# Mixing products of 33 rows and the decay's second product in pairs of row halves, two banks at a time

## The reference, cut to what matters

```
xa = ln(x);  sx = shift(xa) - xa
t  = tanh((xa + sx * maa_x) @ maa_w1).reshape(B, L, 5, 32)
mw, mk, mv, mr, mg = einsum('blfd,fdc->blfc', t, maa_w2)     # five products over only 32 rows
xw = xa + sx * (maa_w + mw)   ... the same for k, v, r, g
w  = exp(-exp(time_decay + tanh(xw @ decay_w1) @ decay_w2))  # the last product is over 64 rows
r, k, v = xr @ Wr.T, xk @ Wk.T, xv @ Wv.T;  g = silu(xg @ Wg.T)
for each token:  a = k v^T;  out = r (faaaa a + s);  s = a + w s
y = groupnorm(out);  x = x + (y * g) @ Wo.T
xc = ln(x);  x = x + sigmoid(xr2 @ fWr.T) * (relu(xk2 @ fWk.T)^2 @ fWv.T)
```

## Time and profile before

| | |
|---|---|
| median of 3 runs | 4260.67 us (4258.37 to 4265.11) |
| the profiled execution | 4252.74 us, its span 4250.9 us |
| busy over the span: TensorE, VectorE | 3730.4 us (88%), 2998.0 us (71%) |
| busy: ScalarE, GpSimd | 2057.8 us (48%), 1742.2 us (41%) |
| mean granted clock of TensorE | 0.954 of 2.4 GHz |

### The profile page before, as it was taken

One profiled execution on the slowest core, in us unless ns is written; L12 is line 12 of the kernel. 1 busy time (PEld: TensorE's weight loads), 2 busy tenths in 40 slices (PEclk: granted clock), 3 DMA queues, 4 the chain that ended last, 5 costly groups with the idle time before them and its releaser, 6 DMA issues. The chain is left out here.

```text
span 4250.9 us, 71399 instructions
## 1 busy us (share of the span) xinstructions
PE 3730.4 (88%) x21636; PEld 2882.3 (68%) x21636; DVE 2998.0 (71%) x6732; ACT 2057.8 (48%) x5384; POOL 1742.2 (41%) x1210
## 2 busy tenths in 40 slices
PE   5998998588888886999999778999999999999976
PEld 4777777477777774899999655666666666666643
DVE  5777777477777775556556338888888878888872
ACT  4777777367777675545545322333333333333322
POOL 2444444144444441000000135666666666666652
PEclk9999999799999997999999889999999999999988
DMA  3434434344444443010010210000000000000000
GB/s 110 104 99 109 104 99 104 96 116 118 104 114 110 122 104 116 30 44 30 30 41 33 73 50 18 24 24 23 24 23 24 23 24 23 24 23 23 23 18 15
DMA packets 146611, 256.58 MB, mean 60 GB/s; under 512 B 27184, under 2 KB 32048, under 8 KB 145424
## 3 DMA queue, kind: packets, MB, share of 16 engines
q1 hardware_dynamic: 146448, 254.49, 22.0%
HBM read 107.62 MB, written 33.55 MB: 33 GB/s over the span
## 5 line engine op out<-in xcount | busy, mean ns | idle before, releaser
L1201 POOL TENSOR_TENSOR c_S<-c_S,c_rT 128x1024 f32<-128x1024 f32 x256 | 558.1, 2180 | 458.4 <-DVE c_S L1479 417.6
L1479 DVE TENSOR_TENSOR_SCAN c_S<-c_wT,c_s,c_vb 128x256 f32<-128x256 f32 x1024 | 709.0, 734 | 45.0 <-issue 2.7
L1474 DVE TENSOR_TENSOR c_vb<-c_kT,c_vb 128x512 f32<-128x512 f32 x512 | 352.4, 688 | 286.4 <-PE c_vb L1645 255.6
L348 POOL TENSOR_TENSOR x_prob<-x_prob,x_rsums 128x512 f32<-128x512 f32 x256 | 275.2, 1075 | 477.7 <-DVE x_rsums L510 477.7
L348 POOL TENSOR_TENSOR s_prob<-s_prob,s_rsums 128x512 f32<-128x512 f32 x256 | 275.2, 1075 | 431.0 <-DVE s_rsums L510 431.0
L1645 PE MATMUL c_vb<-c_vhl,c_spread 128*128 128x512 f32 x512 | 300.4, 597 | 73.6 <-DVE c_S L1479 60.6
L404 ACT ACTIVATE x_prob<-x_t,x_tmin 128x256 f32<-128x256 f32 x512 | 256.4, 502 | 218.3 <-DVE x_tmin L503 218.0
L404 ACT ACTIVATE s_prob<-s_t,s_tmin 128x256 f32<-128x256 f32 x512 | 256.5, 502 | 193.9 <-DVE s_tmin L503 193.6
L862 PE MATMUL b_ps<-b_ln_high,b_w_high 128*128 128x256 f32 x1024 | 290.9, 284 | 14.8 <-DVE b_ln_low L804 14.8
L863 PE MATMUL b_ps<-b_ln_low,b_w_high 128*128 128x256 f32 x1024 | 290.8, 284 | 0.0
L864 PE MATMUL b_ps<-b_ln_high,b_w_low 128*128 128x256 f32 x1024 | 290.8, 284 | 0.0
(11 more groups left out here) (266 smaller groups left out, 10572.4 us busy)
## 6 DMA issues: line engine op xcount, KB each, us to landing
s_stack<-s_parts_qk SPq DMA_DIRECT2D x384, 128.0 KB, 2.4
x_stack<-x_parts_qk SPq DMA_DIRECT2D x384, 128.0 KB, 2.4
s_x_in<-in_x SPq DMA_DIRECT2D x16, 512.0 KB, 3.6
s_xb<-in_x SPq DMA_DIRECT2D x16, 512.0 KB, 4.1
x<-s_x_out SPq DMA_DIRECT2D x16, 512.0 KB, 4.8
x_enc<-in_ctx SPq DMA_DIRECT2D x16, 512.0 KB, 4.4
x_x_in<-x SPq DMA_DIRECT2D x16, 512.0 KB, 3.7
x_xb<-x SPq DMA_DIRECT2D x16, 512.0 KB, 4.1
```

Source lines behind the costliest of these rows:

```text
L348: nc.gpsimd.tensor_tensor(prob[:, h % 4, :, :], prob[:, h % 4, :, :], rsums[:, h, :].unsqueeze(2).to_broadcast([P, TC, T]), ALU.mult).then ...
L1201: nc.gpsimd.tensor_tensor(S[:, n % 4, :, 0:T], S[:, n % 4, :, 0:T], rT[:, par, :, :], ALU.mult).then_inc(z_ready, 1)
L1474: nc.vector.tensor_tensor(pair(vb, i), pair(kT[:, par, :, :], i), pair(vb, i), ALU.mult)
L1479: op = nc.vector.tensor_tensor_scan(S[:, n % 4, c, 1:T + 1], wT[:, par, c, :], vb[:, c, :], s0[:, par, c, n:n + 1], ALU.mult, ALU.add)
```

## The change

It does four things. (1) The pieces of `tT` and `mix2` move: each mixing matrix has 33 rows, and starts at row 0 (w, r, g) or row 64 (k, v); `dec1` writes its result to rows 64 to 127 and `dec2` runs there. (2) Two units, one of each row half (mw with mk, mr with mv, mg with dec2), are issued together by `fill_together`, alternating between two banks. (3) `FILLS` is reordered, so that such units are neighbours: mk joins mw in step 0, k0 and k1 move to the end of step 2 and the start of step 3, mr and mv stand in step 4, mg and dec2 in step 8, xcT and v0 in step 9, g0 in step 11; GpSimd's `sxc` moves from step 8 to 9 and its addition for g from step 7 to 8. (4) `t` is split into 128 and 32 columns, and its tanh is taken in five pieces of 32 rows.

```diff
-    FILLS = {0: (["g1"], ["mw0", "mw1"]), 1: (["mk0", "mk1"], ["y0", "y1"]), 2: (["dec1"], ["mr0", "mr1"]),
-             3: (["k0"], ["dec20", "dec21"]), 4: (["zT0", "zT1"], ["k1"]), 5: (["o0"], ["mv0", "mv1"]),
-             6: (["r0"], ["o1"]), 7: (["r1"], ["mg0", "mg1"]), 8: (["bonus0", "bonus1"], ["xcT0", "xcT1"]),
-             9: (["v0"], []), 10: (["v1"], ["g0"]), 11: (["kk0"], []), 12: (["kk1"], []),
-             13: (["xaT0", "xaT1"], ["rr0"]), 14: (["rr1"], ["kv0"]), 15: (["kv1"], ["t"])}
+    FILLS = {0: (["g1"], ["mw0", "mk0", "mw1", "mk1"]), 1: ([], ["y0", "y1"]), 2: (["dec1"], ["k0"]), 3: (["k1"], []),
+             4: (["zT0", "zT1"], ["mr0", "mv0", "mr1", "mv1"]), 5: (["o0"], []), 6: (["o1"], ["r0"]), 7: (["r1"], []),
+             8: (["bonus0", "bonus1"], ["mg0", "dec20", "mg1", "dec21"]), 9: (["xcT0", "xcT1"], ["v0"]), 10: (["v1"], []),
+             11: (["kk0"], ["g0"]), 12: (["kk1"], []), 13: (["xaT0", "xaT1"], ["rr0"]), 14: (["rr1"], ["kv0"]),
+             15: (["kv1"], ["t"])}
+    TOGETHER = {"mk0": "mw0", "mk1": "mw1", "mv0": "mr0", "mv1": "mr1", "dec20": "mg0", "dec21": "mg1"}
+    MIX_AT = {"w": (0, 0), "k": (2 * DM, 0), "v": (2 * DM, 1), "r": (0, 2), "g": (0, 1)}
...
-                    if n == 8:
+                    if n == 9:
                         pool.wait_ge(emptied["act"], units.emptied(k + 2, "xcT1"))
                         nc.gpsimd.tensor_tensor(sxc[:, :, :], xcT[:, :, 0:T], xcT[:, :, 1:T + 1],
...
-                        if "front" in parts and n in (0, 1, 4, 5, 7):
-                            add_xa(k, MIX[(0, 1, 4, 5, 7).index(n)])
+                        if "front" in parts and n in (0, 1, 4, 5, 8):
+                            add_xa(k, MIX[(0, 1, 4, 5, 8).index(n)])
...
-                        nc.scalar.activation(tT[0:3 * DM, 0, :], unit(name)[0:3 * DM, 0:T], ACT.Tanh)
-                        nc.scalar.activation(tT[0:2 * DM, 1, :], unit(name)[0:2 * DM, T:2 * T], ACT.Tanh).then_inc(done, 1)
+                        for j, n in enumerate("wkvrg"):
+                            row, place = MIX_AT[n]
+                            op = nc.scalar.activation(tT[row:row + DM, place, :], channels(name)[DM * j % P:DM * j % P + DM, DM * j // P, :],
+                                                      ACT.Tanh)
+                        op.then_inc(done, 1)
...
+                def few_rows(name, a):
+                    c = 2 * int(name[-1]) + a
+                    row, place = (DD, 2) if name[:-1] == "dec2" else MIX_AT[name[1]]
+                    if name[:-1] == "dec2":
+                        rows, moving = DD, decT[:, :]
+                    else:
+                        rows, moving = DM + 1, tT[:, place, :]
+                    return nc.tensor.matmul(channels(name)[:, a, :], mix2[row:row + rows, place, c * P:(c + 1) * P],
+                                            moving[row:row + rows, :], start=True, stop=True)
+
+                def fill_together(k, name, second):
+                    if name == "mw0":
+                        pe.wait_ge(emptied["act"], units.emptied(k + 1, "t"))
+                        pe.wait_ge(mix2_loaded, 16 * NMIX * (KC + 1))
+                    if second == "dec20":
+                        pe.wait_ge(emptied["act"], units.emptied(k + 2, "dec1"))
+                        weights("decay_w2")
+                    few_rows(name, 0)
+                    few_rows(second, 0)
+                    few_rows(name, 1).then_inc(filled, 1)
+                    few_rows(second, 1).then_inc(filled, 1)
+
                 def take(k, names, parts, par):
                     for name in names:
                         reader, value = units.before(k + 2, name)
                         pe.wait_ge(emptied[reader], value)
-                        if part_of(name) in parts:
+                        if name in TOGETHER.values() and part_of(name) in parts:
+                            continue
+                        if name in TOGETHER and part_of(name) in parts:
+                            fill_together(k, TOGETHER[name], name)
+                        elif part_of(name) in parts:
                             fill(k, name, 1 - par)
```

More of the change, by code:

```diff
@@ L990, in phase_c @@
         centred = sb("centred", P, 2, P)
-        mix2 = sb("mix2", P, NMIX, C)
-        w = {**w, **{n: sb(n, P, *shape) for n, shape in WEIGHTS_C.items()}}
+        mix2 = sb("mix2", P, 3, C)
+        w = {**w, **{n: sb(n, P, *shape) for n, shape in WEIGHTS_C.items() if n != "decay_w2"}}
         acc = ctx.enter_context(nc.psum_tensor("c_acc", [P, KC, T], F32))
@@ L1085, in load_weight @@
                 def load_weight(n):
-                    rows = d[n].shape[0]
-                    dst = g2T[:, :, :, :].rearrange("p a (c b) n -> p (a c) (b n)", b=2) if n == "Wv" else w[n][0:rows]
+                    dst = mix2[DD:2 * DD, 2, :] if n == "decay_w2" else w[n][0:P]
+                    if n == "Wv":
+                        dst = g2T[:, :, :, :].rearrange("p a (c b) n -> p (a c) (b n)", b=2)
                     sp.dma_start(dst, d[n]).then_inc(weights_loaded[n], 16)
@@ L1092, in _ @@
                 for j in range(NMIX):
-                    place = DM * j if j < 3 else DM * (j - 3)
-                    sp.dma_start(mix2[place:place + DM, j, :],
+                    row, place = MIX_AT["wkvrg"[j]]
+                    sp.dma_start(mix2[row:row + DM, place, :],
                                  d["maa_w2"][DM * j % P:DM * j % P + DM, DM * j // P, :]).then_inc(mix2_loaded, 16)
                     at = COL_AT["maa_" + "wkvrg"[j]]
-                    ones = 3 * DM if j < 3 else 2 * DM
                     for c in range(KC):
-                        sp.dma_start(mix2[ones:ones + 1, j, c * P:(c + 1) * P],
+                        sp.dma_start(mix2[row + DM:row + DM + 1, place, c * P:(c + 1) * P],
                                      d["cols"][:, at + c:at + c + 1].rearrange("p o -> o p"),
@@ L1525, in weights @@
                         pe.wait_ge(weights_loaded[name], 16)
-                    return w[name]
+                    return w.get(name)
                 def transposed(out, src, c):
@@ L1569, in fill @@
                         pe.wait_ge(xxx_ready, k + 3)
-                        for to, n0, n in ((0, 0, 3 * DM), (1, 3 * DM, 2 * DM)):
+                        for to, n0, n in ((0, 0, P), (1, P, NMIX * DM - P)):
                             for c in range(KC):
@@ L1573, in fill @@
                                                       xmix[:, 0, c, :], start=(c == 0), stop=(c == KC - 1))
-                    elif what in ("mw", "mk", "mr", "mv", "mg"):
-                        if name == "mw0":
-                            pe.wait_ge(emptied["act"], units.emptied(k + 1, "t"))
-                            pe.wait_ge(mix2_loaded, 16 * NMIX * (KC + 1))
-                        j = "wkvrg".index(what[1])
-                        rows = 3 * DM + 1 if j < 3 else 2 * DM + 1
-                        for a in range(2):
-                            c = 2 * i + a
-                            op = nc.tensor.matmul(u[:, a, :], mix2[0:rows, j, c * P:(c + 1) * P], tT[0:rows, j // 3, :],
-                                                  start=True, stop=True)
                     elif name == "dec1":
@@ L1586, in fill @@
                         for c in range(KC):
-                            op = nc.tensor.matmul(u[0:DD, 0, :], weights("decay_w1")[:, c, :], xmix[:, 1, c, :],
+                            op = nc.tensor.matmul(u[DD:2 * DD, 0, :], weights("decay_w1")[:, c, :], xmix[:, 1, c, :],
                                                   start=(c == 0), stop=(c == KC - 1))
-                    elif what == "dec2":
-                        pe.wait_ge(emptied["act"], units.emptied(k + 2, "dec1"))
-                        for a in range(2):
-                            c = 2 * i + a
-                            op = nc.tensor.matmul(u[:, a, :], weights("decay_w2")[0:DD, c * P:(c + 1) * P], decT[:, :],
-                                                  start=True, stop=True)
                     elif what == "bonus":
```

6 lines of the change are left out of this document (3 added, 3 removed).

## The result

The changed kernel takes 4428.14 us (median of 4 runs, 4411.97 to 4429.77), the kernel before 4259.76 beside it: ratio 1.0384, 95% interval 1.0358 to 1.0410. The direction was as forecast, the size was not: +168 us where +65 was said, and 50 us above the range.

The account below looks back on a forecast made before the run. No engine bounds it throughout: TensorE's queue is late in about half the steps, VectorE busy through the others. 4.2 us lost plus 0.1 for the clock, over 15 passes, gave +65 and 4325 us; range 4272 to 4378.

Parts of the forecast that it names:

- Overlap of pairs: Mixing products and dec2 in separate row halves run together on TensorE, saving 5.1 us a pass (bounds 0 and 5.1).
- rival "no overlap": Pairs in row halves don't run together; +35 us on the forecast, 4360 us; chance 0.13.
- g1's bank: Step 0: pair 2 and broadcast 1.0 wait for VectorE's read of g1; half 1.0 at +8.2 instead of +6.5.
- k moved ahead: Steps 2 to 5: k0 waits for GpSimd's sum, and k0, k1 hold broadcasts 3.0, 3.1; half 3.1 5.8 us late.
- o0 set by GpSimd's gating: Around half 5.0: o0 waits for GpSimd's gating, late by k's chain, and starts at +35.9.
- Steps 5 to 9 win back 3.1: Products of mv and mg gone from steps 5 to 7, VectorE sets the pace; half 9.0 only 1.4 us late.
- the walk: Step-by-step timing of one pass from g1's first product; loss 4.2 us a pass, perhaps 2.5 too long.
- second chain: Steps 9 to 13: xcT0 waits for mg0's bank, GpSimd's difference moves later; kk0 at +74.1 instead of +70.6.
- Clock, +0.1 us a pass: Idle stretches of TensorE move more than they multiply, so granted clock costs +0.1 us a pass; bounds -0.9 and +1.7.
- rival "clock": Clock falls at k0 and a second place in each pass, 1.7 us each; +51 us, 4376 us; chance 0.12.
- the two terms that could lengthen the time: Upper bounds over 15 passes: no overlap on pair 2 and the mg/dec2 group, +35 us; the clock, +24 us.

Follow-up runs that it names:

- c_order_only: Kernel before with the changed kernel's order of fills and GpSimd's two steps that go with it, each unit as before, no pairs: 4419.09 us, 1.0378.
- i_same_rows: Changed kernel with both partners of each pair in the same row half, so that nothing runs side by side: 4515.07 us, 1.0617.
- p_own_waits: i_same_rows with partners taken apart, each unit waiting for its own bank alone and filled at once: 4502.13 us, 1.0590.
- o_all_rows: i_same_rows with mixing products over 128 rows, 64 for r, zero coefficients in the rows added: 4505.77 us, 1.0586.
- m_pairs_64: Changed kernel with mixing products over 64 rows instead of 33, zero coefficients in the rows added: 4413.59 us, 1.0362.
- b_pair_late: Changed kernel with the second pair of step 0 (mw1, mk1) moved behind broadcast 1.0, to step 1: 4422.69 us, 1.0396.
- e_k_apart: Changed kernel with k0 and k1 each one list later, behind broadcasts 3.0 and 3.1: 4367.70 us, 1.0248.
- a_read_first: Changed kernel with VectorE reading mr and mv ahead of half 5.0 instead of behind it: 4360.96 us, 1.0259.
- g_xct_first: Changed kernel with xcT ahead of mg and dec2 in step 8, and GpSimd's sxc back in step 8: 4385.87 us, 1.0302.
- f_idle_filled: Changed kernel with four full-row products, overwritten afterwards, ahead of the fills of pair 2 and of k0: 4423.15 us, 1.0387.
- r_own_waits_full: p_own_waits with 128 rows for products of w, k, v and r and 64 for g, zero coefficients added: 4396.82 us, 1.0321.

## Why the prediction was wrong

Three differences between runs add up to the 168 us. The order: before to c_order_only, +165. Few rows and filling in groups, still without overlap: c to i_same_rows, +96. The overlap: i to the changed kernel, -92. The last two cancel, which is why the pairs look as if they did nothing.

How the 96 us divide depends on which comes first. Rows first: c to p_own_waits +82, then grouping, p to i, +14. Grouping first: c to o_all_rows +84, of which the switches between 64 and 128 rows may be up to 44, then rows, o to i, +12. Each costs some 80 us alone, and both hardly more. So it is shown that few rows cost 82 to 85 us where each unit waits for its own bank, but not that they cost as much in the changed kernel, which is grouped: there 64 rows instead of 33 give 12 us (m_pairs_64), within the error. What grouping costs by itself was not taken apart.

By the steps of the prediction, in the pass shown (forecast, then measured, from g1's first product):

- *Overlap of pairs*: eight records in 1.13 us and 16 in 2.00. Right, and its worth of 92 us is no less than the 5.1 x 15 = 77 of the ideal, within the error; where the clock is low each record spared is twice as long (0.43 us in the group of p_own_waits above). The rival "no overlap" fell, and its price of 35 us was too low.
- *g1's bank*: half 1.0 +8.2, measured +9.4. The wait is there as described; 1.2 us are pair 2 and its broadcast at 1.2 GHz. The place was right, but b_pair_late removes the wait and gains nothing: the waits of y, dec1 and k0 take it over.
- *k moved ahead*: k0 +20.3, half 3.0 +24.3, half 3.1 +29.1; measured +21.5, +25.5, +30.4. Right but for the 1.2 carried along. e_k_apart shows that this costs 60 us, one of the two largest parts.
- *o0 set by GpSimd's gating*, +35.9: **this step failed.** Gating ended at +37.1, but o0 started at +39.4. o0 takes the bank of mr0, and VectorE reads mr0 only behind half 5.0, because the second list of step 4 is read in step 5. I followed o0's input and not its bank. Of the 3.5 us, 2.3 are this wait; a_read_first gives 62 us back, 4.1 a pass, more than the wait itself, because the low stretch behind it mostly goes with it.
- *Steps 5 to 9 win back 3.1*: half 9.0 +59.6, measured 3256.46, +63.4: the 3.8 us of the steps ahead, nothing more (in eight of the twelve steady passes the clock makes it +66 to +67). From there on the walk was exact: kk0 +74.1 (measured +77.9), half 11.1 +78.1 (+81.8), half 13.1 +89.6 (+93.3), each as late as half 9.0. g_xct_first gives 41 us for this second chain.
- *Clock, +0.1 us a pass*: **the second step that failed.** I took idle time for the only cause, moved the low stretches with the idle stretches, and so found no net change. Low time rose from 141 to 338 us, in a steady pass from 4.8 to 15.1, worth up to half of the 10.3 us. Of the rise of 197, the order alone makes 71 (c_order_only); 64 rows instead of 33 take 44 away again (m_pairs_64), two filled pauses 40 (f_idle_filled). So both idle time and few rows have a share, and the runs don't divide the whole. The rows of before held the hint that I had no price for: its mixing products, over 97 and 65 rows, were to become products over 33, and I counted records and their time, and not how much of the array they use. The rival "clock" (a fall at k0 and a second one, 1.7 us each) had the right sign and one wrong place: the falls came at pair 2, at o0 (1.7 us there, as priced) and at +61.

The Trainium skill ("TensorE: Matmul & The Clock Gate", Part 1, HAM oscillation) puts such falls down to TensorE's pauses between bursts. The traces agree with it in part: in f_idle_filled, which fills pauses, low time is 298 us and not 338. But pauses are not all: p_own_waits and r_own_waits_full have the same pauses ahead of the same group, and the level falls only with 33 rows. Where the two differ, the measurement decides.

Added up for the pass shown: 4.2 forecast and 3.7 more by half 13.1 (1.2 the clock, 2.3 the bank, 0.2 small differences). From one half 0.0 to the next this pass grew by 7.5 us (107.3 to 114.8), the mean of the twelve by 9.3. The eight passes with two more low stretches, at +41 and +61, grew by 10.0 to 10.4, the four others by 7.5 to 8.1: the rest of the steady loss is the clock's too.

Outside the steady passes, passes 0, 13 and 14 lose 12 to 15 us each, not 4.3; their low time rose by 17 to 27 us, a steady pass's by 10, but what starts it was not taken apart. Pass 15, which has no front and was left out of the sum, loses 9 us, of which 4.4 come at half 11.1, behind kk0: the second moved chain runs there too. The range, last: the two terms that could lengthen the time, 35 and 24, reach 4384 us, not 4378; the measured time is above both.

## What to carry to other kernels

When units are reordered, follow each one twice, for its input and for the last reader of the bank that it takes over, with the place that this reader has in its own queue. Packing small products into parts of the array saves their time, but price the rest of the packing too: here few rows and filling in groups cost 96 us, and the overlap gave 92 back. Where products run one after another, each with its own wait, more rows of zeros gained some 85 us and took only memory. A wait can cost more than its length: that for o0's bank cost 2.3 us, and 1.7 more where the clock fell behind it. Where two units are neighbours in different row halves already, their own waits were enough for mg and dec2, and no common one was needed.

## What the runs showed of the hardware

- **The granted clock fell where products used fewer rows.** Same order, same records, zero coefficients added: low time 478 us at 33 rows (4502 us), 216 us at 128 (64 for g; 4397 us, with one group side by side). In the grouped form 479, 393 and 331 us at 33, 64 and 128 rows (64 for r), but there the time moved by only 12 to 17 us.
- **Row halves overlap without being interleaved in the program, and matmuls start out of its order.** In r_own_waits_full, mg0's four records stand ahead of dec20's in the program, yet both sets start within 0.03 us of each other, dec20's first (3251.03) before mg0's second (3251.38). So what is said of the queues at the start, that each runs in order, does not hold strictly for TensorE's. The Trainium skill ("TensorE: Matmul & The Clock Gate", Part 3) tells of a reorder window that loads weights early when they are bound for other rows, and has the matmuls themselves start in program order. The trace agrees with the first and not with the second, and the measurement decides.
- **The wait for a bank can be followed by a clock fall.** Behind a wait of 2.94 us o0 took 5.40 us in pass 8, at a granted clock of 0.59, and 3.70 behind one of 2.95 us in pass 6, where the clock did not fall.
- **A change between 64 and 128 rows costs 0.19 us a product** where the two alternate (group of eight products, 16 records, 5.09 us, 3.61 without).
